# Routing tile by tile inside the attention groups, with the groups written out

## What is computed

```python
h = patches(x) @ W.T + b                       # then the class token in front
h = h + attention(layernorm(layernorm(h)))     # scores - 0.2 * conv3x3(scores), softmax, @ v
x2 = layernorm(h)
logits_fk = (x2 @ W_fk + b_fk) @ normed(emb_fk).T      # 128 logits; the same for rk
w_fk = top4(softmax(logits_fk)), scaled to sum 1       # the same for rk
hid = sum over the 4 experts n of w_fk[n] * (x2 @ f_know[n])   # 192 -> 128
out = h + sum over the 4 experts n of w_rk[n] * (hid @ r_know[n])   # 128 -> 192
```

## Time and profile before

| | |
|---|---|
| median of three runs | 926.44 us |
| profiled execution | 927.07 us, span 925.3 us |
| TensorE busy | 642.7 us (69%) |
| VectorE busy | 382.9 us (41%) |
| ScalarE busy | 344.2 us (37%) |
| GpSimd busy | 374.9 us (41%) |
| mean granted TensorE clock | 0.86 of full speed |

### The profile page before, as it was taken

The page is one execution under the profiler, slowest core; times in us unless marked ns, Lnnn a source line. Parts: engine busy times, 40 slices in busy tenths (PEclk is TensorE's granted clock), DMA queues, the critical chain, the costliest instruction groups (busy, mean ns, idle before and its releaser), DMA issues.

```text
span 925.3 us, 16120 instructions
## 1 busy us (share of the span) xinstructions
PE 642.7 (69%) x4484; PEld 514.2 (56%) x4485; DVE 382.9 (41%) x1370; ACT 344.2 (37%) x738; POOL 374.9 (41%) x381
## 2 busy tenths in 40 slices
PE   3888999999897472075999969998006786778300
PEld 3777887788786351043887858887004554455200
DVE  3537676776766698978900001111111100231032
ACT  3055357436535261053334424344003444344200
POOL 2330332233012001771770037776677710771275
PEclk9979999999999596577899979999557999799755
DMA  5124624643921179911575436665996865676532
GB/s 124 50 56 170 226 59 185 227 166 126 399 115 48 35 155 219 279 66 50 161 199 130 118 103 186 183 185 156 286 337 194 209 161 128 178 213 163 134 98 71
DMA packets 140382, 146.83 MB, mean 159 GB/s; under 512 B 11989, under 2 KB 123902, under 8 KB 140350
## 3 DMA queue, kind: packets, MB, share of 16 engines
q1 hardware_dynamic: 126974, 119.06, 45.0%
q0 software_dynamic: 13376, 27.41, 10.2%
HBM read 73.40 MB, written 73.02 MB: 158 GB/s over the span
## 4 chain that ended last, share of the span: by engine, by line
PE 48%; DVE 15%; DMA 12%; issue 10%; SPq 6%; ACT 5%; POOL 3%; ACTq 1%; POOLq 0%; DVEq 0%
PE bank L945 21%; PE bank L710 8%; DMA wide_dram<-os 7%; PE bank L934 5%; SPq L447 4%; POOL gat L577 3%; PE bank L739 3%; DVE pick L1540 2%; PE bank L788 2%; PE bank L767 2%; DMA xs<-mid_dram 2%; ACT xsT L1157 1%; ACT os L1149 1%; PE bank L699 1%; DMA h_dram<-h 1%
## 5 line engine op out<-in xcount | busy, mean ns | idle before, releaser
L945 PE MATMUL bank<-matrices,xsT 96*64 (+1 forms) x1696 | 253.2, 301 | 16.8 <-ACT xsT L1157 16.5
L945 PEld LDWEIGHTS bank<-matrices,xsT 96*64 96x64 f32 (+1 forms) x1696 | 200.2, 141 | 53.6 <-issue 34.4
L577 POOL DMA_INDIRECT gat<-wide_dram,slots x152 | 146.0, 961 | 186.1 <-SPq L436 140.7
L934 PE MATMUL bank<-ident,xs 128*96 128x128 f32 (+1 forms) x424 | 83.1, 308 | 91.4 <-DMA xs<-mid_dram 64.1
L569 POOL DMA_INDIRECT wide_dram<-x2b,slots x76 | 78.2, 1029 | 116.2 <-issue 95.2
L934 PEld LDWEIGHTS bank<-ident,xs 128*96 128x96 f32 (+1 forms) x424 | 49.5, 165 | 126.9 <-DMA xs<-mid_dram 61.4
L1571 DVE TENSOR_SCALAR acc<-gat,wts 128x128 f32<-128x128 f32 x19 | 6.1, 323 | 247.0 <-DMA gat<-wide_dram,slots 247.0
L527 POOL TENSOR_TENSOR qk_sum<-qk_pad 128x888 f32<-128x888 f32 x16 | 27.7, 1730 | 185.1 <-ACT qk_pad L1025 143.7
L1157 ACT ACTIVATE xsT<-bank 96x512 f32<-96x512 f32 (+1 forms) x140 | 65.2, 485 | 83.3 <-PE bank L934 82.6
L1149 ACT ACTIVATE os<-bank 64x384 f32<-64x384 f32 x136 | 58.4, 478 | 81.0 <-PE bank L945 43.2
L1144 ACT ACTIVATE os<-bank 64x512 f32<-64x512 f32 x72 | 42.6, 591 | 114.9 <-PE bank L945 114.9
(11 more groups left out here) (171 smaller groups left out, 861.0 us busy)
## 6 DMA issues: line engine op xcount, KB each, us to landing
wide_dram<-zeros SPq DMA_DIRECT2D x16, 1248.0 KB, 10.3
xs<-wide_dram SPq DMA_DIRECT2D x72, 192.0 KB
mid_dram<-zeros SPq DMA_DIRECT2D x16, 832.0 KB, 12.4
wide_dram<-os SPq DMA_DIRECT2D x68, 192.0 KB, 2.9
matrices<-in_L_ffn_f_know SPq DMA_DIRECT2D x8, 1536.0 KB, 24.8
matrices<-in_L_ffn_r_know SPq DMA_DIRECT2D x8, 1536.0 KB, 17.2
wide_dram<-os SPq DMA_DIRECT2D x72, 128.0 KB, 2.5
xs<-mid_dram SPq DMA_DIRECT2D x68, 128.0 KB, 3.0
```

Source lines behind the costliest of these rows:

```text
L577: pool.indirect_dma_start(gat[i][:, e, :], None, wide_dram[b], bass.IndirectOffsetOnAxis(ap=slots[:, t, k:k + 1], axis=0))\
L934: last = pe.transpose(bank[r % 2][0:kp, c:c + ROWS], src, ident[:])
L945: last = pe.matmul(out_bank[0:W, n * width:(n + 1) * width], xsT[r % 2][0:kp, c:c + W], matrices[0:kp, bass.ds(starts[(r * SB + k) * 2 + h ...
```

## The change

Each group's tiles of 128 tokens that are complete are reloaded right after the group's store. Tiles per group from group 0 on: 2, 2, 2, 3, 2, 2, 3, 3. `attention(g)` works on the tiles that group g-1 completed (`tiles_of(g)`: none, 0-1, 2-3, 4-5, 6-8, 9-10, 11-12, 13-15): normalise, transpose, logits, top entries. Their rank matmuls come in attention(g+1). The batches are now tiles 0 to 8 and 9 to 18. The plan of batch 0 lies in attention(5), its slots in attention(5), (6) and (7), and its scatters behind them on GpSimd. After attention(7) come tiles 16 to 18, the plan of batch 1, and its ten slots and scatters. The hardware loops over the groups are gone, each group is written out. The logit bias moves into the matmul as a row of ones. The products of `attend` use two banks in turn. The per-tile routing buffers (`logit`, `hot`, `x2T` and the small ones) have three copies in place of two. The wide buffers are cleared in groups 0 to 2 and 3 to 5.

TensorE, the order inside a group:

```diff
+            def attention(g):
+                ...
                 scores(g, 0)
                 scores(g, 1)
+                if n_old > 0:
+                    ranks_before(old[0])
                 if more > 0:
                     turn_xn(g + 1)
                 turn(g, 0)
                 scores(g, 2)
                 if more > 0:
                     project(g + 1, 0)
+                if n_old > 0:
+                    ranks_after(old[0])
+                if n_old > 1:
+                    ranks_before(old[1])
                 turn(g, 1)
                 scores(g, 3)
                 if more > 0:
                     project(g + 1, 1)
+                if n_old > 1:
+                    ranks_after(old[1])
+                if n_old > 2:
+                    ranks_before(old[2])
                 attend(g, 0)
                 turn(g, 2)
+                if n_old > 2:
+                    ranks_after(old[2])
                 attend(g, 1)
                 turn(g, 3)
+                if planned:
+                    plan(0, 0)
                 attend(g, 2)
+                for t in ts:
+                    route_transpose(t)
                 if more > 0:
                     project(g + 1, 2)
+                if planned:
+                    plan(0, 1)
                 attend(g, 3)
+                for t in ts:
+                    route_logits(t)
+                if planned:
+                    plan(0, 2)
                 if more > 1:
                     for s in range(2):
-                        to_pixels(g + 2, ring, s)
+                        to_pixels(g + 2, s)
                     for j in range(TILES):
                         embed(g + 2, j, False)
```

VectorE (`weights` is the sum, reciprocal and product of the top-4 weights; `token_factors` now also takes the statistics and waits for the reload):

```diff
                 for f in range(3):
+                    if f < len(ts):
+                        route_top(ts[f])
                     values(g, f)
                     if embedding:
                         newton(g + 1, f)
...
+            def attention(g):
+                ...
                 softmax_in(g, 0)
                 softmax_in(g, 1)
+                if old:
+                    weights(old)
                 softmax_in(g, 2)
                 softmax_in(g, 3)
                 finish(g, 0)
+                if planned:
+                    plan(0, 0)
                 finish(g, 1)
                 finish(g, 2)
+                if planned:
+                    plan(0, 1)
                 finish(g, 3)
                 if more > 0:
                     cat(g + 1, 0)
                     queries(g + 1)
                     if more > 1:
                         cat(g + 1, 1)
+                    if planned:
+                        plan(0, 2)
-                    prepare(g + 1, more > 1)
+                    prepare(g + 1, more > 1, ts)
+                else:
+                    for t in ts:
+                        route_top(t)
+                if planned:
+                    plan(0, 3)
+                for t in SLOTTED.get(g, []):
+                    slot(0, t)
+                token_factors(g + 1)
```

with `SLOTTED = {5: [0, 1, 2], 6: [3, 4, 5, 6], 7: [7, 8]}`. SyncE:

```diff
+            for g in range(GROUPS):
+                if g + 3 < GROUPS:
+                    load_lines(g + 3)
                 zero_slots(g)
                 store_group(g)
+                reload(g)
```

More of the change, by code:

```diff
@@ L792, in attend, with route_transpose @@
                 last.then_inc(pv_done, 1)
-            def attention(g, more):
-                ring = 4 + RING_USES * (g + 1) + 2
+            def route_transpose(t):
+                u = RING_USE["turned", t, 0]
+                pe.wait_ge(x2t_ready, t + 1)
+                pe.wait_ge(ring_emptied, u + 1)
+                src = x2b[:, t, :] if t < BATCHES[0][1] else x2t[t % 3][:]
+                for j in range(2):
+                    last = pe.transpose(bank[u % 2][0:DH, j * ROWS:(j + 1) * ROWS], src[:, j * DH:(j + 1) * DH], ident[:])
+                last.then_inc(ring_filled, 1)
@@ new lines, in route_logits, with ranks @@
+            def route_logits(t):
+                u = RING_USE["logits", t, 0]
+                pe.wait_ge(x2T_copied, t + 1)
+                pe.wait_ge(ring_emptied, u + 1)
+                pe.wait_ge(one_row, 1)
+                pe.matmul(bank[u % 2][:, 0:256], x2T[t % 3][:, 0, :], r_mat[:, 0, :], start=True, stop=False)
+                pe.matmul(bank[u % 2][:, 0:256], x2T[t % 3][0:DH, 1, :], r_mat[0:DH, 1, :], start=False, stop=True)\
+                  .then_inc(ring_filled, 1)
+            def ranks(t, mat, done):
+                first = t in (BATCHES[0][0], BATCHES[1][0])
+                for e in range(TOPK):
+                    last = pe.matmul(bank[3][:, 0:256], mat[:], hot[t % 3][:, :, e, :],
+                                     start=first and mat is before and e == 0, stop=False, skip_group_check=True)
+                last.then_inc(done, 1)
@@ new lines, in ranks_before, with ranks_after, plan @@
+            def ranks_before(t):
+                pe.wait_ge(hot_ready, t + 1)
+                if t == BATCHES[1][0]:
+                    pe.wait_ge(plan_ev[0], 4)
+                ranks(t, before, rank_filled)
+            def ranks_after(t):
+                pe.wait_ge(rank_copied, t + 1)
+                ranks(t, after, hot_used)
+            def plan(b, part):
+                pe.wait_ge(plan_ev[b], part + 1)
+                if part == 0:
+                    for r in range(2):
+                        last = pe.matmul(bank[3][:, r:r + 1], upto[:], nblk[:, r:r + 1], start=True, stop=True)
+                elif part == 1:
+                    for r in range(2):
+                        last = pe.matmul(bank[3][:, r * 128:(r + 1) * 128], ones[:], diag[:, r, :], start=True, stop=True)
+                else:
+                    for r in range(2):
+                        last = pe.matmul(bank[3][0:1, r * BLOCKS:(r + 1) * BLOCKS], ones_bf[:], passed[:, r, :],
+                                         start=True, stop=True)
+                last.then_inc(plan_ps, 1)
@@ L1562, in combine @@
+            for g in range(GROUPS):
+                attention(g)
+            last_tiles, end_tiles = tiles_of(GROUPS - 1), tiles_of(GROUPS)
+            weights(last_tiles)
+            for t in end_tiles:
+                route_top(t)
+            weights(end_tiles)
+            for part in range(4):
+                plan(1, part)
+            for t in range(*BATCHES[1]):
+                slot(1, t)
             def combine(layer, t):
```

696 lines of the change are left out of this document (357 added, 339 removed).

## The result

| | before | changed |
|---|---|---|
| median of four runs each | 926.32 us (925.67 to 928.57) | 1003.76 us (999.71 to 1008.58) |
| profiled execution, span | 925.3 us | 1006.9 us |
| TensorE busy / mean granted clock | 642.7 us / 0.86 | 672.7 us / 0.808 |
| VectorE busy | 382.9 us | 393.1 us |

The change makes the kernel slower: 1.082 times the time before, 95% interval 1.077 to 1.087.

The account below looks back on a forecast made before the run. The routing chain after attention was taken as the bound: 102.5 us put ahead, 44.5 returned. Then 58.0 + 8 (clock) - 10.9 + 0.5 + 5.1 (experts, tail) = 60.7 us on 927.07, median 987, range 957 to 1007.

Parts of the forecast that it names:

- The joint: Embedding's end to next group's first transpose: TensorE waits for VectorE, so added work costs 8.6 us (two tiles), 11.4 (three).
- the rival that counted on it (910): Attention groups: routing fills VectorE's 10 free us, only the excess is paid; total 910 us, chance 0.08.
- The plan's stall: Group 5: TensorE idles 8.7 us before the pixels, as VectorE's plan part stands behind cat(6, 1).
- Slots: Batch 0's slots on VectorE in groups 5 and 6: 2.84 us each, 8.5 for three, 11.4 for four.
- Written-out code: Group loops written out: no instruction fetch on the chain, taken as 0 us, bounds -2 to +5.
- The bound behind T: After attention's last h2 write: the matrices' load replaces routing as bound; first expert matmul 78 us later, plan about 48.
- T: Time of the last h2 write ending attention: 317.90 us before, forecast 420.4, 102.5 later, without the clock term.
- The clock: TensorE's half-clock restarts after new waits in groups 5 and 6: 8 us, bounds 2 and 25.
- half clock in every joint: Rival: TensorE at half clock after every embedding-to-transpose stretch, or unseen waits between engines; total 1000 to 1015 us, chance 0.15.
- The experts: Expert phases: eight layer-1 steps for batch 0 instead of nine, -10.9 us; layer 2 +0.5; tail +5.1.

Follow-up runs that it names:

- the experiment: Changed kernel with VectorE's third part of batch 0's plan moved ahead of the next group's cat; 1.016 times the kernel before, TensorE's stall 0.35 us instead of 8.34.
- the filled kernel: Changed kernel with useless matmuls added where TensorE waits between the embedding's end and the next group's first transpose; 1.044 times the kernel before.

## Why the prediction was right, and where not

**The joint: right.** Forecast 9.0 + 8.6 = 17.6 for two tiles, measured 17.5, 17.5 and 17.9 (groups 1 to 3); with three tops 20.4 and 19.7; with three slots and the last part of the plan 27.4 and 27.1. Free time of VectorE over a group hid none of it, and the rival that counted on it (910) is out.

**The plan's stall: right**, 8.7 and 8.34, and the experiment took it away. **Slots: right**, 8.5 for three and 8.6 in their joint; 19.9 for seven and 22.6 in the intervals, with what they do to the clock. **Written-out code: right**, nothing.

**The bound behind T: right.** The matrices take over at T + 79.7 (78), and the plan is done at T + 44.9 (48).

**The clock: mis-sized.** The term that was mis-sized is "I take 8 us, bounds 2 and 25". Everything to T together came out 8.1 over the forecast with its 8. I add up by how much TensorE's rows in the changed kernel outside the joints are longer than the same rows at full clock: 4.4 behind the joint between groups 0 and 1 (scores x12 in 2.21 in place of 1.23, projections and transposes alike), 4.8 in three embeddings (9.75 twice and 9.53 in place of 8.07), 3.5 in group 5, 4.9 in group 6, 2.6 in group 7, together some 20 us, and 22 with the value products ahead of group 7. In the kernel before the same sum is some 7 us. The difference, 13 to 15, is 5 to 7 more than my 8 and most of what was missing. It holds for the profiled execution: as said, the same instructions took 5 us less in another one, so the term is some 8 to 15 us. I had charged three long waits, in groups 5 and 6, and nothing for the pieces of 2 to 4 us in the other joints; the experiment with a busy TensorE shows that these lower the clock too. Nor has a restart a fixed price. The 3 us are right for the first expert matmuls of the kernel before, where two sets of sixteen take 3.68 and 3.28 us in place of 1.96; here a restart cost 4.4 behind one joint and, outside the joint, nothing behind the next three. By the Trainium skill's rule ("TensorE: Matmul & The Clock Gate", section "HAM oscillation — how this bites in real kernels") all seven joints pay, 21 us. That is 6 to 8 over the rows' 13 to 15, about as far off as my 8 is under: after three of the joints the group's rest runs at full clock (granted clock 1.00 from 162.7 to 181.7, 207.3 to 226.2 and 253.8 to 274.0), so not every joint pays outside itself. The rival "half clock in every joint", 1000 to 1015, names this cause, and the median (1003.8) lies in its span; but half clock in every joint, as it says, is more than the rows show.

**The experts: mechanism right, a size off.** Eight steps in the first phase: the expert matmuls of both layers are x1632 in place of x1696 (a step of layer 1 is 64). In this execution layer 1 still gained only 2.3: behind the start of its second phase TensorE ran 30 us at half clock, at a time when it was busy 25.8 of them. The window, and then TensorE at the start of that phase in the changed kernel:

```profile
606.00:636.00 30.00, 25.76 (x110) 21.36 (x111) 4.22 (x12) 6.65 (x12) 22.13 (x23) 0.50 0.52 141
```

```profile
609.12 1.10 PE L997 MATMUL bank<-ident,xs 128*96 128x128 f32 x4 [6.58 <-DMA xs<-wide_dram]
...
635.60 3.68 PE L1008 MATMUL bank<-matrices,xsT 96*64 x16
```

And in the kernel before:

```profile
546.05 1.10 PE L934 MATMUL bank<-ident,xs 128*96 128x128 f32 x4 [6.63 <-DMA xs<-wide_dram]
...
548.88 3.68 PE L945 MATMUL bank<-matrices,xsT 96*64 x16
552.49 1.10 PE L934 MATMUL bank<-ident,xs 128*96 128x128 f32 x4
553.52 1.96 PE L945 MATMUL bank<-matrices,xsT 96*64 x16
```

Both kernels wait 6.6 us there. Before, one set of sixteen matmuls ran at half clock behind it; now six sets did, one every 4.6 us in place of every 2.5. Five more such sets are some 10 us, which is about the missing 8.6. Why the clock stayed low so much longer behind an equal wait is open. Layer 2 took 3.0 more than forecast, the tail 0.6 less. Whether the other three executions (4.3 to 8.9 us under the profiled one) had the same stretch is open.

**What stays open.** The clock's share in groups 6 and 7 is only added up from rows, not tested. Why the expert stages are so much slower on the chips of the experiments was not tried. In those profiles TensorE sits idle 164 to 185 us ahead of the expert matmuls, where it was 16 and 17 us in the first two, and "another core or an unknown queue" holds 13 to 18% of the chain, with no such entry in the first two.

## What to carry to other kernels

Before work is moved into an engine's free time, find where in the period that time lies: here VectorE had 10 of 32 us free and none of it in the stretch where TensorE waits for it, so seven joints paid every instruction in full. A move pays only if the stage it leaves was the last to arrive by as much: 118.6 us were put in front and 42.7 came back, because the matrices' load became the bound at once. And when a wait is lengthened for TensorE, price the half clock behind it too, from short waits as well: here it was 8 to 15 us.

## What the runs showed that I had not expected

- A store with 37 rows outermost holds the reload back for 12.0 us; the same bytes as 36 + 1 rows for 3.3 us.
- TensorE falls to half clock in busy stretches too: in the filled kernel an embedding takes 9.75 us in place of 8.07, at a granted clock of 0.83, with no wait over 1.32 us in the 17 us ahead of it; in the kernel before three embeddings are lengthened so.
- Removing work from a joint can bring less than adding it cost: 1.0 us against 3.2 in a joint with two tops, where two removals worth 0.8 and 1.0 alone bring 4.0 together; in joints with none, with three tops or with slots the same removal brought all of its 3.2.
- The same instructions, up to the store of group 5, took 230.1 us in one execution and 224.7 in another, by where TensorE's clock fell.
- One and the same kernel took 1004 us in the first runs and 1196 on another chip or at another time, with six of its seven intervals in the attention equal to 0.1 us. The change cost 77 us in the one case and 25 in the other.
